# Step tables packed into one word, VectorE's pick one-hots two groups ahead, own rows by a transfer (two-layer graph network on one core)

## The reference

```python
h = relu(layernorm(x))
# layer 0: messages into the target, then a GRU cell
msg = h[src] @ W_msg.T + b_msg + edge_embed[edge_type]
x = x + gru(segment_sum(msg, dst), h)
# layer 1: every node collects the rows of its edges' other ends
h = relu(layernorm(x))
agg = segment_sum(h[dst], src)
z = ((1 + eps) * h + agg) @ W1.T + b1
x = x + relu(batchnorm(z)) @ W2.T + b2
```

## Time and profile before

| what | us |
|---|---|
| median of 3 runs (5647.15 to 5655.27) | 5654.18 |
| the profiled execution's own time | 5650.5 |
| its span, first to last instruction | 5648.7 |
| busy: TensorE matmul / VectorE / ScalarE / GpSimd | 3221.0 / 2670.9 / 1608.2 / 3336.2 |
| GpSimd in gathers (1664) / in scatters (1664) | 1576.9 / 1631.5 |
| mean granted TensorE clock, share of full speed | 0.644 |

### The profile page before, as it was taken

One profiled execution on the slowest core, in us unless ns is written; L12 is line 12 of the kernel. 1 busy time (PEld: TensorE's weight loads), 2 busy tenths in 40 slices (PEclk: granted clock), 3 DMA queues, 4 the chain that ended last, 5 costly groups with the idle time before them and its releaser, 6 DMA issues.

```text
span 5648.7 us, 78171 instructions
## 1 busy us (share of the span) xinstructions
PE 3221.0 (57%) x17495; PEld 2607.6 (46%) x17496; DVE 2670.9 (47%) x4799; ACT 1608.2 (28%) x3266; POOL 3336.2 (59%) x3510
## 2 busy tenths in 40 slices
PE   4566666666666665665943333333335666666767
PEld 3344444444444444444733222322324565556656
DVE  7566665666665656664641011111003444445557
ACT  4323222222222322222432222222222222221137
POOL 0666666666666666665136666666666666655563
PEclk8555555555555555555975555555556888878889
DMA  4222222222222111111222222222223444445455
GB/s 144 79 69 67 68 66 68 67 67 67 69 68 66 54 44 43 44 44 39 65 74 74 71 71 74 74 71 74 70 71 128 159 161 146 154 152 174 175 186 181
DMA packets 311629, 514.05 MB, mean 91 GB/s; under 512 B 68678, under 2 KB 227065, under 8 KB 295517
## 3 DMA queue, kind: packets, MB, share of 16 engines
q0 software_dynamic: 106944, 226.05, 13.4%
q1 hardware_dynamic: 118669, 242.40, 13.0%
q10 hardware_dynamic: 85904, 44.17, 2.6%
HBM read 331.72 MB, written 180.64 MB: 91 GB/s over the span
## 4 chain that ended last, share of the span: by engine, by line
another core or an unknown queue 33%; PE 25%; issue 20%; DVE 9%; ACT 5%; ACTq 2%; DVEq 2%; POOL 1%; DMA 1%; SPq 0%; POOLq 0%
PE ps L1700 6%; PE ps L1715 6%; PE ps L1569 4%; PE ps L1583 3%; PE ps L1591 2%; DVE sb_Y L1356 2%; ACT sb_counts L740 2%; DVE sb_blks L1157 2%; PE ps L1739 2%; ACT sb_ring L852 1%; ACTq L848 1%; PE ps L1712 1%; DVEq L1165 1%; DVE sb_oh L1146 1%
## 5 line engine op out<-in xcount | busy, mean ns | idle before, releaser
L649 POOL DMA_INDIRECT rows_by_src<-sb_ring,sb_posE x1664 | 1631.5, 980 | 966.1 <-ACT sb_ring L852 485.3
L626 POOL DMA_INDIRECT sb_ring<-msg_table,sb_stepE x1664 | 1576.9, 948 | 1034.6 <-SPq L466 498.6
L1700 PE MATMUL ps<-sb_H,sb_oh 128*128 x3520 | 725.0, 367 | 1161.9 <-issue 517.6
L1700 PEld LDWEIGHTS ps<-sb_H,sb_oh 128*128 128x128 f32 x3520 | 620.3, 263 | 1265.6 <-issue 1263.8
L1569 PE MATMUL ps<-sb_ring,sb_oh 128*128 x3520 | 926.9, 435 | 216.8 <-issue 208.4
L1569 PEld LDWEIGHTS ps<-sb_ring,sb_oh 128*128 128x128 f32 x3520 | 779.0, 319 | 310.0 <-issue 306.0
L1338 DVE TENSOR_SCALAR sb_oh<-sb_oh,sb_cf 128x512 f32<-128x512 bf16 x440 | 215.4, 503 | 1212.4 <-remote 933.9
L852 ACT COPY sb_ring<-ps 128x512 f32<-128x512 f32 x416 | 242.8, 584 | 1913.0 <-remote 1308.1
L740 ACT CAST sb_counts<-ps 54x512 bf16<-54x512 f32 x440 | 254.8, 579 | 1757.3 <-remote 1198.7
L1189 DVE TENSOR_TENSOR sb_Y<-sb_Y,ps 128x512 f32 x440 | 300.0, 682 | 636.6 <-remote 576.6
L1583 PE MATMUL ps<-sb_oh,sb_toh 128*54 128x128 bf16 x1760 | 320.0, 301 | 261.2 <-issue 252.3
(11 more groups left out here) (225 smaller groups left out, 3855.2 us busy)
## 6 DMA issues: line engine op xcount, KB each, us to landing
sb_stepE<-rows_by_src SPq DMA_DIRECT2D x114, 1088.0 KB
sb_oh<-step_targets SPq DMA_DIRECT2D x110, 512.0 KB
rows_by_src<-sb_cf ACTq DMA_DIRECT2D x294, 136.0 KB
sb_ring<-msg_table,sb_stepE POOLq DMA_INDIRECT x1664
rows_by_src<-sb_ring,sb_posE POOLq DMA_INDIRECT x1664
sb_ring<-rows_by_src SPq DMA_DIRECT2D x11, 1088.0 KB, 5.1
msg_table<-sb_oh SPq DMA_DIRECT2D x14, 448.0 KB, 3.2
sb_oh<-in_x SPq DMA_DIRECT2D x49, 128.0 KB, 2.1
```

What stands on the lines that cost most here:

```text
L626: pool.indirect_dma_start(out=ring[:, m % RGROUPS * G + q, 0:F], out_offset=None, in_=table_d[:, :], in_offset=bass.IndirectOffsetOnAxis(a ...
L649: pool.indirect_dma_start(out=rows_d[:, :], out_offset=bass.IndirectOffsetOnAxis(ap=posE[:, m * G + q:m * G + q + 1], axis=0), in_=ring[:, ...
L1700: m = mm(picked_ps[:, ds(slot, P)], pick[g][:, q * P:(q + 1) * P], H[:, ds(off, P)], start=False, stop=True, skip_group_check=True)
```

## The change

1. Offset, slot and tile count of a step go into one 32-bit word. For layer 0 it is the tile's number shifted by 9 with the relative offset below it, for the picks the number shifted by 14 with the absolute offset. VectorE makes both tables early (`step_words`), SyncE stores and reloads them, and TensorE loads 16 words a chunk (`load_words`), in group 1 of the chunk before, into two sets of registers. The fields are taken out of the word by masks and shifts on TensorE's sequencer; the tile count of a group comes from the word of its last step.
2. VectorE makes the pick one-hots two groups ahead of the sums beside which it made them (`PICKS_AHEAD`).
3. SyncE copies the pair of blocks that `h2T` transposes into `own_buf`, 128 KB, two chunks ahead (`own_in`); TensorE reads it at a fixed address.
4. TensorE's picks no longer have straight pairs except single ones between loops; the plan gets one more cut before the last whole pair of own rows.

```diff
-    plan, at = [(0, 1, None, 0, 0), (1, turns, None, 0, 0), (turns, turns + 1, None, 0, 0)], turns + 1
+    plan, at = [(0, 1, None, 0, 0), (1, turns - 1, None, 0, 0), (turns - 1, turns, None, 0, 0),
+                (turns, turns + 1, None, 0, 0)], turns + 1
...
-T_BLOCK, T_SLOT, T_NEED, T_PICK, T_END = 0, SB, 32, 32 + SB, 64
+T_BLOCK, T_TILE, T_END = 0, SB, 32
...
+        own_buf = [type_rows[:, k, 0:2 * GW].bitcast(f32) for k in range(2)]
...
             def tables_in():
+                sp.wait_ge(S("words_made"), 1)
+                sp.dma_start(words_d.rearrange("w s p -> s w p"),
+                             early_i[0:SB, P:3 * P].rearrange("s (w p) -> s w p", w=2)).then_inc(S("row_out_d"), 16)
                 sp.wait_ge(S("row_out_d"), 32)
                 sp.dma_start(steprow, table_row(T_BLOCK, STEPS_P)).then_inc(S("steprow_in"), 16)
-                sp.dma_start(slotrow, table_row(T_SLOT, STEPS_P)).then_inc(S("steprow_in"), 16)
-                sp.dma_start(needrow, needs_d.rearrange("(o a) b -> o (a b)", o=1)[:, 0:GROUPS]).then_inc(S("steprow_in"), 16)
+                sp.dma_start(wordrow, word_row(0)).then_inc(S("steprow_in"), 16)
                 sp.dma_start(endrow, table_row(T_END, TGROUPS)).then_inc(S("steprow_in"), 16)
...
-            sp.dma_start(slotrow, table_row(T_PICK, STEPS_P)).then_inc(S("steprow_in"), 16)
+            sp.dma_start(wordrow, word_row(1)).then_inc(S("steprow_in"), 16)
...
+            def own_in(c, k):
+
+                wait(sp, "h2_ps", c - 1)
+                sp.dma_start(own_buf[k], H[:, ds(c * GW, GW)]).then_inc(S(f"own_in{k}"), 16)
+
+            sp.wait_ge(S("h2_act"), ACT_BLOCKS // 2)
+            sp.wait_ge(S("h2_vec"), VGROUPS)
+            own_in(0, 0)
+            own_in(1, 1)
...
+                if own and not (isinstance(c, int) and c + 2 >= TURNS):
+                    own_in(c + 2, k)
...
+            def step_words():
+
+                dve.wait_ge(S("tables_kept"), 1)
+                off = tables_i[T_BLOCK:T_BLOCK + SB, :]
+                first = off.rearrange("s (g q) -> s g q", q=G)[:, :, 0:1].to_broadcast([SB, P // G, G])
+                vs.tensor_tensor(step_rel.rearrange("s (g q) -> s g q", q=G), off.rearrange("s (g q) -> s g q", q=G), first,
+                                 ALU.subtract)
+                vs.tensor_scalar(msg_words, step_tile, 9, None, ALU.logical_shift_left)
+                link(vs.tensor_scalar(pick_words, step_tile, 14, None, ALU.logical_shift_left))
+                vs.tensor_tensor(msg_words, msg_words, step_rel, ALU.bitwise_or)
+                vs.tensor_tensor(pick_words, pick_words, off, ALU.bitwise_or).then_inc(S("words_made"), 1)
...
+                last = isinstance(j, int) and j * 2 + k == CHUNKS - 1
                 for p in range(GPC):
-                    layer1_pick(j, k, p)
+                    if p < GPC - PICKS_AHEAD:
+                        layer1_pick(j, k, p + PICKS_AHEAD)
+                    elif not last:
+                        layer1_pick(j + k, 1 - k, p + PICKS_AHEAD - GPC)
...
+            for g in range(PICKS_AHEAD):
+                layer1_pick(0, 0, g)
...
+            words = [[pe.alloc_register(f"step_word{k}_{q}") for q in range(CH)] for k in range(2)]
             sum_regs = [pe.alloc_register(f"sum_off{q}") for q in range(CH)]
 
-            def step_offsets(c, row=steprow):
-                nc.tensor.load(regs, row[0:1, ds(c * CH, CH)])
-
-            def step_slots(c):
-                nc.tensor.load(slots, slotrow[:, ds(c * CH, CH)])
-
-            def wait_tiles(name, n):
-
-                pe.wait_ge(S(name), pe.value_load(needrow[:, ds(n, 1)], min_val=1, max_val=TGROUPS))
-
-            def rel(g, q, regs=regs):
+            need = pe.alloc_register("step_need")
+
+            def load_words(c, k):
+                nc.tensor.load(words[k], wordrow[:, ds(c * CH, CH)])
+
+            def word(k, s, top):
+                return pe.snap(words[k][s], min_val=0, max_val=top)
+
+            def within(value, top):
+                return nc.s_assert_within(pe.snap(value), 0, top, skip_runtime_bounds_check_because="a field of a step's word")
+
+            MSG_TOP, PICK_TOP = (TILES << 9) - 1, (TILES << 14) - 1
+
+            def wait_tiles(name, value):
+
+                pe.reg_alu(need, pe.snap(value + 1), 1, ALU.max)
+                pe.wait_ge(S(name), pe.snap(need, min_val=1, max_val=TGROUPS))
+
+            def msg_rel(k, s):
+                return within(word(k, s, MSG_TOP) & 511, (s % G) * P)
...
-                    o = bank(1 + g)[:, 0:P] if q == 0 else ps[:, 1 + g, ds(rel(g, q), P)]
-                    tile = pe.snap(slots[s], min_val=0, max_val=(2 * CH - 1) * RW)
-                    mm(o, oh[:, k, s, :], ringf[:, ds(tile, F)], start=False, stop=True, skip_group_check=True)
+                    o = bank(1 + g)[:, 0:P] if q == 0 else ps[:, 1 + g, ds(msg_rel(k, s), P)]
+                    slot = within((word(k, s, MSG_TOP) >> 9) & (2 * CH - 1), 2 * CH - 1)
+                    mm(o, oh[:, k, s, :], ringf[:, ds(slot * RW, F)], start=False, stop=True, skip_group_check=True)
...
-                    wait_tiles("tiles_in", n)
+                    wait_tiles("tiles_in", word(k, g * G + G - 1, MSG_TOP) >> 11)
                     sum_rows(g, k, n)
+                    if g == 1 and not (isinstance(c, int) and c == CHUNKS - 1):
+                        load_words(c + 1, 1 - k)
                     add_types(g, n)
...
-            def h2T(c, k):
-
+            def h2T(j, k):
+
+                c = j * 2 + k
+                pe.wait_ge(S(f"own_in{k}"), j * 16 + 16)
                 wait(pe, "h2_done", c - 1)
                 for b in range(NG):
-                    m = nc.tensor.transpose(bank(4 + k)[:, b * P:(b + 1) * P], H[:, ds(c * GW + b * P, P)], ident)
+                    m = nc.tensor.transpose(bank(4 + k)[:, b * P:(b + 1) * P], own_buf[k][:, b * P:(b + 1) * P], ident)
                 m.then_inc(S("h2_ps"), 1)
...
-                    h2T(c, k)
-                step_offsets(c)
-                step_slots(c)
+                    h2T(j, k)
                 if first == 0:
                     pe.wait_ge(S("h2_done"), TURNS)
                 for g in range(GPC):
                     n = c * GPC + g
-                    wait_tiles("bank_clear", n)
+                    wait_tiles("bank_clear", word(k, g * G + G - 1, PICK_TOP) >> 16)
                     pe.wait_ge(S("pick_oh"), n + 1)
                     for q in range(G):
-                        off = pe.snap(regs[g * G + q], min_val=0, max_val=(BLOCKS - 1) * P)
-                        slot = pe.snap(slots[g * G + q], min_val=0, max_val=(CH - 1) * P)
-                        m = mm(picked_ps[:, ds(slot, P)], pick[g][:, q * P:(q + 1) * P], H[:, ds(off, P)],
+                        off = within(word(k, g * G + q, PICK_TOP) & ((1 << 14) - 1), (BLOCKS - 1) * P)
+                        slot = within((word(k, g * G + q, PICK_TOP) >> 14) & (CH - 1), CH - 1)
+                        m = mm(picked_ps[:, ds(slot * P, P)], pick[g][:, q * P:(q + 1) * P], H[:, ds(off, P)],
                                start=False, stop=True, skip_group_check=True)
                     m.then_inc(S("picked"), 1)
+                    if g == 1 and not (isinstance(c, int) and c == CHUNKS - 1):
+                        load_words(c + 1, 1 - k)
...
-            pick_loop(pe, picks_and_sums, TURNS // 2)
+            load_words(0, 0)
+            pick_loop(pe, picks_and_sums)
```

More of the change, by code:

```diff
@@ L269, in build_gnn @@
         tile_f, tile_i = small(SB), small(SB, i32)
-        slot_i, pslot_i, need_i, end_i = small(SB, i32), small(SB, i32), small(SB, i32), small(G, i32)
+        end_i = small(G, i32)
         tables_f = sb("tables_f", [P, TABR])
         early_i = blk1hf.bitcast(i32)
-        tables_i, needs_i = early_i[0:TABR, 0:P], early_i[:, P:P + P // G]
+        tables_i = early_i[0:TABR, 0:P]
+        msg_words, pick_words, step_rel, step_tile = (early_i[0:SB, a * P:(a + 1) * P] for a in range(1, 5))
         end_f, tile_thr, tiles_at = small(G), small(G), small(G)
```

53 lines of the change are left out of this document (27 added, 26 removed).

## The result

| | before | changed |
|---|---|---|
| median of 3 runs, us | 5654.18 | 6163.13 (6157.35 to 6172.54) |
| ratio, 95% interval | | 1.0906 [1.088, 1.0932] |
| span of the profiled execution | 5648.7 | 6155.5 |
| mean granted clock | 0.644 | 0.61 |

The account below looks back on a forecast made before the run. GpSimd's indirect transfers were taken to set the floor, with TensorE's work partly on the path. Terms -85 + 27 + 35 + 3 = -20 us on 5650.5 gave 5630, stated as 5632; range 5510 to 5760, likeliest case 5590 to 5680.

Parts of the forecast that it names:

- GpSimd's floor: Layer 0 and picks: GpSimd issues one gather every 1.25 us when nothing stops it, so 18.9 us a chunk at least.
- the rhythm of eight: Layer 0: GpSimd issues eight gathers, then stands 2.19 us, 208 times, 471.9 us in all.
- The coupling: Signals of TensorE arrive late while GpSimd issues without a break; all move on once it has stopped.
- the price of the masks: Layer 0: masks and shifts plus the sequencer's lost lead cost 0.28 us a group, 1.1 a chunk.
- the 0.45 of TensorE's time: Layer 0: share of TensorE's saved time that shortens a chunk near GpSimd's floor; -1.9 us a chunk gives -94, taken as -85.
- The loads: Layer 0: removing the loads at a chunk's start saves 2.4 us a chunk, the groups' own tile-count loads 1.8.
- Picks without sums: 64 chunks: net +2.1 us of sequencer a chunk, priced at 0.2, gives +27 us; ends 0 and +134.
- Picks with sums: 46 chunks: +2.1 us less 0.7 for the look-ahead, at 0.55, gives 0.8 a chunk, +35 us; ends -46 and +97.
- Own rows by a transfer: 49 transfers of 128 KB before TensorE's transposes: only the first shows, about +3 us; ends 0 and +4.
- The loop: TensorE's picks as 22 passes of a loop instead of 24 straight pairs: cost 0.
- rival 4: Loops wait for their instructions, one to two 1.5 us packets a pass: +107 to +213 us, about 5790; chance 0.03.
- Rival 1: Masks decide: layer 0 gives 0, fewer pick groups stand ready, +132 us, about 5785; chance 0.25.

Follow-up runs that it names:

- e4_rel_early: The kernel before with ready relative offsets, tile counts in a group's first step and loads behind row or pick matmuls: 5625.39 us, ratio 0.9952.
- e1_unpacked: The kernel before with look-ahead, own rows by a transfer and TensorE's picks as one loop, without packed words: 5661.18 us, ratio 1.0018; repeated, 1.0021.
- e2_spare: The kernel before with four idle register instructions at each later row step of layer 0, 48 a chunk: 6012.75 us, ratio 1.0639.
- s2_spare24: The kernel before with two idle register instructions at each later row step of layer 0, 24 a chunk: ratio 1.0072.
- after_again: The changed kernel once more, unaltered, in a set where the kernel before took 4791 us: 4884.09 us, ratio 1.0191.

## Why the prediction was wrong

- **What bounds the kernel.** Right in its parts: GpSimd's floor, the rhythm of eight, signals that come late. The coupling was called unexplained, and still is; it turned out to be there in some sets of runs and not in others.
- **The failing step** is the price of the masks: "I take 0.28 us a group for both, 1.1 a chunk", and behind it the 0.45 of TensorE's time that was to show. 48 instructions that do nothing cost 3.2 us a chunk of whole time (355/110), and the change's +54 net cost 308.5/110 = 2.8. The text knew that the sequencer crawls at times ("the maxima of 725 ns") and used it only to take 9 us off the gain. What it missed: once the crawl has set in, it falls on whatever instructions are left in the cycle, so that 54 more of them multiply the slow ones, 103 to 734. The ends given for layer 0, 0 and -209, held no loss at all.
- **The loads.** Taking them away was to save 4.2 us of TensorE's time a chunk. Without the transfers in the way some of it shows (gaps down by 2.3 us net, perhaps in part by slower matmuls). Inside the rhythm it is worth 0.2 us of the chunk's length, by e4_rel_early, not 0.45 of 4.2. One linear price between stretches cannot serve for a quantity with a knee: near 0 on one side, over 1 on the other.
- **Picks without sums.** +27 us forecast, end +134. The scatters grew by 197.2 us, of which 24.5 - 21.9 = 2.6 us on 64 chunks are 166. The same step failed: 2.1 us of sequencer time was priced at 0.2 of itself, and cost more than all of itself.
- **Picks with sums.** +0.8 us a chunk forecast, 25.4 - 24.6 = 0.8 and 28.0 - 27.4 = 0.6 measured. How far this is luck is open: with two sums e1_unpacked takes 750/(465/15.13) = 24.4 us a chunk, so the look-ahead gave 0.2 us where 0.55 x 0.7 = 0.4 was counted, and in a set of the second kind the change costs 0.9 us with two sums (580/(421/15.13) against 570/(433/15.13)) and about 6 with three. The wait for pick one-hots, 131.9 us in the earlier trace rows, is no longer listed in 4900 to 5450 us, and one for key one-hots stands there, as foretold:

```profile
PE ps L1764 <- DVE sb_stepE L1378: 38.9, 20, 6.1
```

- **Own rows by a transfer.** Cheap, as forecast, but not for the number given. TensorE's wait for the first transfer is 23.8 us, beside others that were there anyway, and three later waits at the picks, 14.4 us in all, are put down to it. The stretch between the stages grew by 3.0 us, the forecast's +3, but e2_spare and s2_spare24, which lack the transfer, have 237.1 and 236.9 us there against the changed kernel's 236.3. The match is luck. Where the trace has the landing (after_again), the transfer takes 4.1 us in the median, 2.1 to 4.3, against a chunk of 19 us or more.
- **The loop, and rival 4.** e1_unpacked bears out the 0: it is 0.2% slower with the loop and the two other parts. Packets of q8 are 54 in the whole changed kernel (62 before), 2 of them in 900 us of the looped picks. Of the fetch at a taken branch that the Trainium skill states (Runtime: NRT & Kernel Launch, "Instruction fetch mechanics") this trace again shows no cost.
- **Rival 1** (the masks decide, in fewer groups per cycle) named the mechanism and the direction: "TensorE must work through 22 instructions a pick group instead of 9". It was priced at 5785, with layer 0 at 0, a quarter of what happened. Its bound should have come from the maxima: 54 instructions at up to 0.7 us are 38 us a chunk, and a tenth of that, a share picked only to show the scale, is 3.8 us on 110 chunks, 418 us, more than the whole range.
- **The sum.** Its terms give 5630 + 4 = 5634 us and not 5632; it changes nothing.

## What to carry to other kernels

Packing fields into a word trades one load for several register instructions a step, and the sequencer's instructions are not free: look at the maxima of their durations, not only the medians, and take runs with a dozen and with a few dozen idle ones to see how far off the knee is. A table that holds each number in the form in which it is used, loaded behind queued matmuls, is the cheaper way. Time a change in more than one set of runs, on more than one chip, before believing its size: this one is 9.1% in one kind of set and 1.9% in the other, in different stages. And look in the trace whether an experiment did what it was built for: a pause that fits into an idle gap paces nothing.

## What the runs showed of the hardware

- In some sets of runs, and not in others, TensorE's sequencer took up to 1.4 us for a register instruction of 32 ns while indirect transfers of GpSimd followed one another. In the changed kernel 734 instructions over 600 ns stood in the middle three quarters of layer 0, in a set of the other kind none. With a quarter of the gathers there was none, and with all gathers but 20 instructions a chunk fewer (e4_rel_early) there was none either.
- The same kernel took 5628 to 5666 us in the sets of one kind and 4786 to 4801 us in those of the other, 15% less, with the granted clock nearly the same (0.644 and 0.654). One chip's number stands in both.
- GpSimd left 0.30 us idle between two indirect transfers. A memset of 174 ns and its wait fitted in: the interval went from 1.25 to 1.28 us.
- With three of four gathers left out, the kernel before ran layer 0 at a granted clock of 0.76 and the changed kernel at 0.54, with the same matmuls to do and 15.9 and 16.3 us a chunk. Whether the clock changed the gaps or the gaps the clock is not shown.
